# First pair of a DLRM tower cut into two quarters and a half, second pair at full width, no warming matmuls

## The reference, cut to what matters

```
x0 = e                                   # 512 x 32 x 16, gathered rows
for W in (W0, W1, W2):                   # W0: 32 x 32 x 64, the others 32 x 64 x 64
    xk = relu(einsum('bmd,bhd,mhk->bkd', x0, xk, W))
    outs.append(sum(xk, axis=2))
h = relu(concat(outs, dense_ctx) @ W_top1 + b_top1)      # 208 -> 512
y = relu(h @ W_top2 + b_top2) @ W_top3                   # 512 -> 256 -> 1
```

## Time and profile before

| what | value |
|---|---|
| median of three runs | 440.99 us |
| the profiled execution | 440.44 us |
| its span | 438.6 us |
| TensorE busy | 325.1 us (74%), 1892 passes |
| VectorE busy | 277.5 us (63%), 174 instructions |
| GpSimd busy | 259.6 us (59%), of it 122.1 in 128 gathers |
| ScalarE busy | 52.4 us (12%) |
| mean granted TensorE clock | 0.887 of full |

### The profile page before, as it was taken

How to read it: one execution, slowest core, us unless ns; L and a number is a source line. 1 busy time by engine, 2 the same in 40 slices (tenths; PEclk the granted TensorE clock), 3 DMA queues, 4 the chain that set the end, 5 groups by cost and what they waited for, 6 DMA issues and landing times.

```text
span 438.6 us, 4843 instructions
## 1 busy us (share of the span) xinstructions
PE 325.1 (74%) x1892; PEld 142.7 (33%) x1892; DVE 277.5 (63%) x174; ACT 52.4 (12%) x71; POOL 259.6 (59%) x199
## 2 busy tenths in 40 slices
PE   5500000028988999935989988998999999999997
PEld 5400000014544555612533332342233333223334
DVE  0000000005779797916899989999898897899911
ACT  1000000000000100100222211211022121121011
POOL 5777777500050000870788998889899878797200
PEclk9955555557999999985999999999999999999999
DMA  5356653000071000991497969897928998904000
GB/s 177 68 176 213 168 150 79 5 1 0 1 228 54 1 0 7 273 324 43 95 296 256 305 159 321 295 307 221 284 56 261 308 374 279 315 21 109 0 1 2
DMA packets 32529, 68.36 MB, mean 156 GB/s; under 512 B 5498, under 2 KB 12026, under 8 KB 32506
## 3 DMA queue, kind: packets, MB, share of 16 engines
q1 hardware_dynamic: 22074, 55.46, 38.1%
q10 hardware_dynamic: 6336, 11.54, 9.4%
q0 software_dynamic: 4096, 1.06, 2.9%
HBM read 54.40 MB, written 1.84 MB: 128 GB/s over the span
## 4 chain that ended last, share of the span: by engine, by line
PE 41%; another core or an unknown queue 22%; DMA 11%; issue 9%; DVE 7%; POOL 7%; ACTq 1%; SPq 1%; ACT 1%; DVEq 0%; POOLq 0%
PE acc L857 30%; DVE vz L659 7%; POOL pz L607 4%; PE factor L824 4%; DMA fields_sb<-fields 3%; POOL gathered L581 3%; DMA hidden<-relu_out 2%; PE factor L802 2%; DMA fields<-gathered 2%; DMA opposite<-fields 2%; DMA rotated<-fields 1%; PE factor L869 1%; ACTq L766 1%; PE factor L864 1%
## 5 line engine op out<-in xcount | busy, mean ns | idle before, releaser
L659 DVE TENSOR_TENSOR vz<-fields_sb,factor 128x1024 f32<-128x1024 f32 (+3 forms) x111 | 224.7, 2070 | 32.7 <-remote 12.9
L857 PE MATMUL acc<-vz,w_sb 128*64 128x512 f32 (+1 forms) x1200 | 225.5, 510 | 21.6 <-DVE vz L659 13.6
L607 POOL TENSOR_TENSOR pz<-fields_sb,hidden 128x1024 f32<-128x1024 f32 (+1 forms) x60 | 132.6, 2234 | 73.1 <-ACT hidden L738 59.7
L581 POOL DMA_INDIRECT gathered<-in_table,index x128 | 122.1, 954 | 72.7 <-DVE vz L670 37.4
L857 PEld LDWEIGHTS acc<-vz,w_sb 128*64 128x64 f32 x1200 | 85.6, 140 | 144.2 <-issue 103.1
L676 DVE TENSOR_TENSOR vz<-own,factor 128x512 f32<-128x512 f32 x8 | 5.5, 688 | 99.1 <-ACT own L730 92.5
L857 PE MATMUL acc<-pz,w_sb 128*64 128x512 f32 (+1 forms) x240 | 57.1, 566 | 2.8 <-POOL pz L607 2.8
L824 PE MATMUL factor<-gathered,unit_sb 32*128 32x128 f32 x32 | 4.2, 342 | 67.5 <-remote 65.9
L755 ACT ACTIVATE relu_out<-acc 128x512 f32<-128x512 f32 (+1 forms) x30 | 15.4, 513 | 146.0 <-PE acc L857 112.9
L724 ACT ACTIVATE factor<-hidden 128x1024 f32<-128x1024 f32 x22 | 22.6, 1028 | 72.0 <-DMA hidden<-relu_out 56.2
L857 PEld LDWEIGHTS acc<-pz,w_sb 128*64 128x64 f32 x240 | 17.3, 137 | 34.6 <-issue 23.9
(11 more groups left out here) (34 smaller groups left out, 63.5 us busy)
## 6 DMA issues: line engine op xcount, KB each, us to landing
fields_sb<-fields SPq DMA_DIRECT2D x48, 512.0 KB
rotated<-fields SPq DMA_DIRECT2D x24, 512.0 KB
hidden<-relu_out ACTq DMA_DIRECT2D x44, 256.0 KB
fields_sb<-fields SPq DMA_DIRECT2D x32, 256.0 KB
own<-fields SPq DMA_DIRECT2D x6, 512.0 KB
gathered<-in_table,index POOLq DMA_INDIRECT x128
fields<-gathered SPq DMA_DIRECT2D x12, 128.0 KB
w_sb<-in_w SPq DMA_DIRECT2D x2, 512.0 KB
```

What stands on the lines that cost most here:

```text
L581: nc.gpsimd.indirect_dma_start(gathered[:, pair % GRING, j, :], None, table, bass.IndirectOffsetOnAxis(ap=index[:, i:i + 1], axis=0)).then ...
L607: nc.gpsimd.tensor_tensor(pz[:, at % PRING, 0:cols], fields[s][:, t, col:col + cols], hidden_of(step, g), ALU.mult).then_inc(pz_ready, 1)
L659: nc.vector.tensor_tensor(vz[:, at:at + nt, 0:cols].rearrange("p t (a n) -> p t a n", n=half), src[:, t:t + nt, col:col + cols].rearrange( ...
L857: last = nc.tensor.matmul(acc_of(step, ab), w_sb[layer][:, kt, :], z[:, ab * half:(ab + 1) * half], start=start and j == 0, stop=stop and ...
```

## The change

It changes lists and constants, the table of factors of a direct block, and the order of the matmuls of the top.

- Pair 0 becomes three blocks: two of 256 columns (4 gathers each) and one of 512 (8 gathers). Pair 1 becomes one block of 1024 columns. There are still ten blocks and four direct ones.
- A direct block of 1024 columns has factor entries of its own, `[(OWN,), (0,), (1,), (2,), (3,), (ACROSS,)]`, and its layer 0 is five products of one tile. The entry that holds only `ACROSS` has no wave 0.
- `BEGUN`, `SPREAD`, `POOL_TILES`, `FIRST_GATHERS` and `GATHERS_IN` are written anew. POOL's tiles fall from 56 to 50, counted in tiles of 1024 columns.
- `WARMING` goes from 30 to 0 and `IN_FLIGHT_DIRECT` from 6 to 4.
- The top's matmuls that don't need layer 2 all come before the wait for `sums_done`, and the others follow in plain order.
- On the host the ids are laid out for the new blocks.

```diff
-BLOCKS = [(pair, half * N, N, half * GATHERS // 2, GATHERS // 2) for pair in range(2) for half in range(2)]
-BLOCKS += [(pair, 0, PAIR, 0, GATHERS) for pair in range(2, PAIRS)]
+BLOCKS = [(0, 0, N // 2, 0, GATHERS // 4), (0, N // 2, N // 2, GATHERS // 4, GATHERS // 4),
+          (0, N, N, GATHERS // 2, GATHERS // 2)]
+BLOCKS += [(pair, 0, PAIR, 0, GATHERS) for pair in range(1, PAIRS)]
...
-BEGUN = [(0, 0), (1, 0), (0, 1), (2, 0), (1, 1), (0, 2), (2, 1), (1, 2), (0, 3), (2, 2), (1, 3), (0, 4),
-         (2, 3), (0, 5), (1, 4), (1, 5), (0, 6), (2, 4), (2, 5), (0, 7), (1, 6), (1, 7), (2, 6), (0, 8),
+BEGUN = [(0, 0), (0, 1), (1, 0), (1, 1), (0, 2), (2, 0), (2, 1), (1, 2), (0, 3), (2, 2), (1, 3), (0, 4),
+         (2, 3), (0, 5), (1, 4), (1, 5), (0, 6), (2, 4), (0, 7), (2, 5), (1, 6), (1, 7), (2, 6), (0, 8),
          (2, 7), (0, 9), (1, 8), (1, 9), (2, 8), (2, 9)]
...
-SPREAD = [(1, 0), (2, 0), (1, 1), (2, 1), (1, 2), (2, 2), (1, 3), (2, 3), (1, 7)]
-POOL_TILES = {(1, 0): 0, (2, 0): 0, (1, 1): 0, (2, 1): 0, (1, 2): 0, (2, 2): 4, (1, 3): 0, (2, 3): 4,
-              (1, 4): 4, (1, 5): 4, (2, 4): 2, (2, 5): 4, (1, 6): 4, (1, 7): 4, (2, 6): 5, (2, 7): 6,
-              (1, 8): 6, (1, 9): 6, (2, 8): 4, (2, 9): 3}
-FIRST_GATHERS = 27
-GATHERS_IN = {(2, 2): (43, 0, 0, 1), (0, 4): (12,), (2, 3): (0, 1, 0, 0), (1, 4): (4, 2, 1, 0),
-              (1, 5): (1, 1, 0, 2), (0, 6): (3,), (2, 4): (1, 1), (2, 5): (5, 2, 3, 1), (0, 7): (5,),
-              (1, 6): (3, 1, 2, 1), (1, 7): (0, 4, 0, 0), (2, 6): (1, 0, 0, 0, 0)}
+SPREAD = [(1, 0), (1, 1), (2, 0), (2, 1), (1, 2), (2, 2), (1, 3), (2, 3)]
+POOL_TILES = {(1, 0): 0, (1, 1): 0, (2, 0): 0, (2, 1): 0, (1, 2): 0, (2, 2): 0, (1, 3): 0, (2, 3): 2,
+              (1, 4): 5, (1, 5): 2, (2, 4): 4, (2, 5): 4, (1, 6): 3, (1, 7): 2, (2, 6): 5, (2, 7): 6,
+              (1, 8): 4, (1, 9): 6, (2, 8): 4, (2, 9): 3}
+FIRST_GATHERS = 32
+GATHERS_IN = {(0, 4): (41,), (2, 3): (6, 0), (0, 5): (5,), (1, 4): (0, 1, 3, 0, 0), (1, 5): (4, 0),
+              (0, 6): (4,), (2, 4): (0, 1, 2, 1), (0, 7): (1,), (2, 5): (7, 0, 1, 0), (1, 6): (0, 0, 3),
+              (1, 7): (1, 8), (2, 6): (4, 3, 0, 0, 0)}
...
-WARMING = 30
+WARMING = 0
...
-IN_FLIGHT_DIRECT = 6
+IN_FLIGHT_DIRECT = 4
...
+            if BLOCKS[b][2] == PAIR:
+                return [(0, t, 1) for t in range(L0TILES + 1)]
             return [(0, 0, 1), (0, 1, 2), (0, 3, 1), (0, L0TILES, 1)]
...
-    units = [(0, t, 2) for t in range(0, TILES, 2)] if b in DIRECT else [(0, 0, 3), (0, 3, 3), (0, 6, 2)]
+    units = [(0, 0, 3), (0, 3, 3), (0, 6, 2)] if BLOCKS[b][2] == PAIR else [(0, t, 2) for t in range(0, TILES, 2)]
...
-            if spread_from_gathered(step):
+            if spread_from_gathered(step) and direct_factors(step[1])[g] != (ACROSS,):
...
-DIRECT_FACTORS = [(OWN, 0), (1, 2), (3, ACROSS)]
+def direct_factors(b):
+    if BLOCKS[b][2] == PAIR:
+        return [(OWN,), *((t,) for t in range(L0TILES)), (ACROSS,)]
+    return [(OWN, 0), (1, 2), (3, ACROSS)]
...
-            for m in range(F_TOP1 // P):
-                row = slice(m * HROWS, (m + 1) * HROWS)
-                nc.tensor.matmul(top1_bank(m), wt1_dense_sb[row, :], dense_sb[row, :], start=True, stop=False)
-            top1_first(0)
-            top1_first(1)
+            for m in range(F_TOP1 // P):
+                nc.tensor.matmul(top1_bank(m), wt1_sb[:, m * P:(m + 1) * P], stack01, start=True, stop=False)
+            for m in range(F_TOP1 // P):
+                row = slice(m * HROWS, (m + 1) * HROWS)
+                nc.tensor.matmul(top1_bank(m), wt1_dense_sb[row, :], dense_sb[row, :], start=False, stop=False)
             pe.wait_ge(sums_done, len(ORDER))
-            for ab in range(2):
-                top1_half(ab, ab).then_inc(top1_wave, 1)
-            top1_first(2)
-            pe.wait_ge(top1_wave, 2)
...
+            for m in range(0, F_TOP1 // P, 2):
+                for ab in range(2):
+                    top1_half(m + ab, ab).then_inc(top1_wave, 1)
+            for m in range(0, F_TOP1 // P, 2):
+                pe.wait_ge(top1_wave, m + 2)
+                for ab in range(2):
+                    top1_half(m + 1 - ab, ab).then_inc(top1_ps, 1)
...
```

More of the change, by code:

```diff
@@ L199, in factor_entry, with factor_entries, factor_used @@
     if spread_from_gathered(step):
[L200 removed]
+        g = next(e for e, held in enumerate(direct_factors(step[1])) if t in held)
     return step, g
[L205 to L209 removed]
+def factor_entries():
+    entries = []
+    for step, u in VECTOR:
+        if spread_from_gathered(step) and u == 0:
+            entries.append((step, 0))
+        entries.append(factor_entry(step, u))
+    return list(dict.fromkeys(entries))
+FACTORS = factor_entries()
+def factor_used(entry):
+    return max((i + 1 for i, (step, u) in enumerate(VECTOR) if factor_entry(step, u) == entry),
+               default=VECTOR.index((entry[0], 0)) + 1)
+FACTOR_USED = [factor_used(entry) for entry in FACTORS]
 def factor_free(entry):
@@ L421, in slot_of @@
         def slot_of(step, held):
-            g = next(e for e, of in enumerate(DIRECT_FACTORS) if held in of)
+            held_by = direct_factors(step[1])
+            g = next(e for e, of in enumerate(held_by) if held in of)
             half = BLOCKS[step[1]][2] // 2
-            at = DIRECT_FACTORS[g].index(held) * half
+            at = held_by[g].index(held) * half
             return factor[FACTORS.index((step, g)) % FRING][:, :, at:at + half]
@@ L678, in direct_product @@
                     return
-                both = factor[FACTORS.index((step, 1)) % FRING][:, :, :].rearrange("p a (t n) -> p t a n", t=2)
+                both = factor[FACTORS.index((step, 1)) % FRING][:, :, 0:2 * half].rearrange("p a (t n) -> p t a n", t=2)
                 nc.vector.tensor_tensor(vz[:, at:at + nt, 0:cols].rearrange("p t (a n) -> p t a n", n=half),
@@ L810, in spread_gathered @@
                 rows, quarter = quarter_rows(b), BLOCKS[b][2] // QUART
-                if wave:
+                if wave and (step, g) in WAVES:
                     pe.wait_ge(wave_done, WAVES.index((step, g)) + 1)
@@ L816, in spread_gathered @@
                         pe.wait_ge(vz_ready, factor_free((step, g)))
[L817 removed]
+                for held in direct_factors(b)[g]:
                     if held == ACROSS:
@@ new lines, in _ @@
+            for m in range(0, F_TOP1 // P, 2):
+                pe.wait_ge(top1_wave, m + 2)
+                for ab in range(2):
+                    top1_half(m + 1 - ab, ab).then_inc(top1_ps, 1)
+            for j in range(0, F_TOP1 // P, 2):
+                for k in range(j, j + 2):
+                    pe.wait_ge(top1_done[k], 1)
+                    last = nc.tensor.matmul(factor[2][:, 0, :], wt2_sb[:, k, 0:P], top1[:, k, :],
+                                            start=k == 0, stop=k == F_TOP1 // P - 1)
+                if j:
+                    last.then_inc(top2_ps, 1)
+                for h in range(2):
+                    for k in range(j, j + 2):
+                        last = nc.tensor.matmul(top2_bank(1, h), wt2_sb[:, k, P:2 * P], top1[:, k, half_batch(h)],
+                                                start=k == 0, stop=k == F_TOP1 // P - 1)
+                    if j:
+                        last.then_inc(top2_ps, 1)
@@ L953 @@
     ids = np.array(inputs["ids"]).reshape(PAIRS, QUART, GATHERS, FIELDS)
-    for pair in {BLOCKS[b][0] for b in DIRECT}:
-        ids[pair] = (ids[pair].reshape(2, 2, 2, GATHERS // 2, FIELDS).transpose(0, 2, 1, 3, 4)
-                     .reshape(ids[pair].shape))
+    samples = ids.reshape(PAIRS, 2, 2 * GATHERS, FIELDS)
+    ids = ids.copy()
+    for pair, _, _, j, rows in BLOCKS:
+        for q in range(QUART):
+            at = 2 * j + q % 2 * rows
+            ids[pair, q, j:j + rows] = samples[pair, q // 2, at:at + rows]
     ids = np.ascontiguousarray(ids.transpose(1, 3, 0, 2).reshape(P, PAIRS * GATHERS))
```

36 lines of the change are left out of this document (1 added, 35 removed).

## The result

The change makes the kernel **slower**: 450.34 us median of 4 runs (448.55 to 453.29) against 440.86 us (438.72 to 441.04), ratio 1.0233 with a 95% interval of 1.0163 to 1.0303. The profiled execution took 448.99 us, its span is 447.2 us (before 438.6).

The account below looks back on a forecast made before the run. It took the kernel as bound by a 97 us opening, where long rows of gathers delay TensorE's completions, then by TensorE, sharing with VectorE in 240 to 320 us. From 440.4 us, -5 - 4 + 2 + 2 = -5 gave 435, range 408 to 446.

Parts of the forecast that it names:

- Later gathers: Gathers after the first 64: rows of nine, six and five cost 6.5 in place of 10.4 us; -4, bounds -9 and +3.
- rival C: Nine gathers right after pair 0's layer 0 stall more, on small blocks: slower, 447 us, 452 at worst; chance 0.10.
- Warming: The 60 warming passes before any data: they cost nothing by themselves, so dropping them counts 0.
- Opening: First 97 us: completions still crawl, but the first quarter's layer 0 is nearly done by then; -5, bounds 0 and -20.
- blocks: Smaller and larger blocks in pairs 0 and 1: two quarters in place of a half; +2 us, bounds 0 and +6.
- head start: First block needs four gathers, not eight: TensorE starts at about 10.5 us, with about 59 passes by 97.1 us.
- Tiles to VectorE: Six full tiles moved from POOL cost VectorE 6.8 us, about half hidden: +2 us, bounds 0 and +6.8.
- Top: Matmuls before the wait for `sums_done`: same work in another order, 0, bounds -0.5 and +0.7 us.
- Rival A: TensorE runs freely during the gathers, work starting at 11 in place of 97 us: 365 us; chance 0.13.

Follow-up runs that it names:

- b_burst15b: On chip 1, kernel before with the row of 6 gathers after pair 0's layer 0 made 15 and the later 12 cut to 4: 441.29 us, 1.0060.
- b_warm0: On chip 1, the kernel before with WARMING = 0 and nothing else: 433.44 us, 0.9831 of the kernel before.
- experiment 2: Chip 1: kernel before again 441.41 us, changed kernel again 449.56, kernel before without warming 433.44, changed kernel with paced gathers 389.97.
- experiment 5: Chip 15: kernel before without warming and with paced gathers 345.28 us, changed kernel unchanged 352.14 us, against the kernel before at 343.98 us.
- before_copy: The kernel before, unchanged, run again on chip 1: 441.41 us, 1.0007 of the kernel before.
- after_copy: The changed kernel, unchanged, run again on chip 1: 449.56 us, 1.0193 of the kernel before.
- b_burst15: On chip 12, kernel before with the row of 6 gathers after pair 0's layer 0 made 15 and the later 12 cut to 4: 357.41 us, 1.0348.
- after_copy2: The changed kernel, unchanged, run on chip 15: 352.14 us, 1.0194 of the kernel before.
- a_late: On chip 14, the changed kernel with twelve of its last gathers moved earlier: 455.2 us, 1.0361 of the kernel before.
- b_pacelin_w0: On chip 1, the kernel before with WARMING = 0 and its gathers from the 17th to the 83rd paced by VectorE's products: 383.89 us, 0.8770.

## Why the prediction was wrong

The forecast was 435 us, in a range of 408 to 446; it came out at 450.34, slower and outside the range. By its own terms:

- **Later gathers: this is the step that failed.** Predicted: nine, six and five gathers at 4.5, 1 and 1 us, 6.5 in place of 10.4, so -4. What the earlier trace rows gave, 0.17 us per gather in a row of six and 0.78 in one of twelve, is not a price per gather. The row of six was nearly free; the row of twelve is 14.8 us long, and its step takes 13.0 us longer than on chip 15 (20.9 against 7.9); the two rows of nine and six are 19.1 us long together, and the kernel is 20.6 us late behind them. What eight or nine cost wasn't measured. And nine and six were counted as two rows. They are parted by one product of 0.73 us (132.24 us), and together they left TensorE idle 16.1 us. That the product doesn't part them is my reading of this one case; the unbroken fifteen of b_burst15b, 18.5 us long, made their step 13.5 us longer. In its place stands a balance: this row against the twelve at 184 us, 20.6 - 11.3 = 9.3 us for the worse by the third line, where the quarters' part is also in. I had the place right (rival C: the nine gathers after pair 0's layer 0, "where nine gathers cost over 6 us") but gave it 14 us at most and a chance of 0.10.
- **Warming: 0 predicted, -7.6 measured** (b_warm0). The prediction even said that the passes fill whatever holds completions back, and then priced that at nothing. If my reading of experiment 2 is right, sixty completions that nobody reads stand in the same line as those that matter. This is the gain of the kernel before; in the changed kernel the going of the warming wasn't tested alone, and the slow first passes of experiment 5 are its other side.
- **Opening -5 and blocks +2: -1.7 together.** With warming's -6.2 (124.2 us in before_copy, 118.0 in b_warm0, at the first line of the table) the quarters cost about +4.5 there, +5.7 in the repeat (before_copy and after_copy are 0.5 us apart), inside my bounds of 0 to +6 but not my +2. "Half of that and a part of its waits is saved" was wrong, since a quarter's layer 0 took as long as a half's. I had also read "80 to 76" instructions of VectorE for pairs 0 and 1: the lists give 70 products in both kernels, so the 0.6 us saved was nothing. The head start itself was seen: wave 0 started at 12.67 us, not at my 10.5, since the fourth gather's rows took 4.53 us to land and not 2.04. 24 passes were started by 17 us and 38 more by 84 us, 62 in all, then none until 96; my 59 by 97 us was nearly right. VectorE's first product came at 36.98 us, but the second at 59.76 and the third at 87.47.
- **Tiles to VectorE: right in size, nothing in time.** VectorE's busy time rose from 277.5 to 283.7 us, +6.2 for the 6.8 said, and POOL's fell by 15.2. Between the third and the fourth line of the table, where I had put +2, the kernel after is 4.2 us faster.
- **Top: 0 predicted, -0.7 measured**, inside the bounds.
- **Not foreseen: the last gathers.** +5.8 us at the step (+7.0 on chip 15), +3.9 at the end (+5.3), but only +0.5 in the repeat, after_copy against before_copy; some 3 us by the medians of experiment 5. The last gather comes 8 us later, and I had looked at the rows only, not at what waits for the last of them. The chain behind it (copy to DRAM, `rotated`, fields of block 8) was there to be read in the code.

Rival A, free running, and the Trainium skill's rule behind it (SBUF — State Buffer, Who interferes with whom) need a remark. On chips 12 and 15 the trace agrees with it: 79 and 73 gathers in a row (b_burst15, after_copy2), TensorE at nine tenths for most of it. In the first result and on chips 1 and 14 it doesn't: 11.83 and 8.46 us of waiting for nobody beside fifteen gathers (11.52 and 8.47 in after_copy, 11.71 and 8.49 in a_late), gone when they are spaced out. Whether what is held back there has to do with the ports that this section is about, no run shows. And rival A wouldn't have paid even where it holds, since there the kernel before runs freely too.

## What to carry to other kernels

When a wait grows with a row of other instructions, price the whole row as it will stand after the change, with rows parted by a short product counted as one until shown otherwise, and not by a mean per instruction; and set it against the row that goes. When work is reordered, follow the last item of each list to who needs it. A smaller first block pays only if its passes get cheaper, so price them from rows at the speed that TensorE has there; here the spreading passes did not, and the whole of it ran at the slow pace. The version that held on both kinds of chip is the kernel before without warming and with its gathers spaced by waits: 0.877 where there are stalls and 1.0036 where there are none.

## What the runs showed of the hardware

- The same program takes 344 us on two chips and 440 us on three (if the first result's is a third), with intervals of a few us. The difference is the stall beside indirect gathers. What differs between the chips is open. One thing goes with it in all runs: on chips 12 and 15 the profile has the landing times of the full tiles of `fields_sb` (5.6 to 6.5 us) and of the gathers (3.6 to 4.5 us), and on chips 1 and 14, as in the first result, it has none for them. It goes with the kind of chip; nothing here says that it is a cause.
- Whether the held-back thing is TensorE's completion, or the semaphore's update, or the wait's release, wasn't told apart: each shows as a late release of VectorE.
- On a stalling chip the paced gathers still cost: b_pacelin_w0 takes 383.89 us there and 345.28 us on chip 15. The row of twelve stays whole in it (127.66 to 141.45 us) and VectorE waits 9.00 us beside it; block 3's layer 1 takes 20.0 us there and 7.9 on chip 15. So 12 of these 39 us are that stall. How the rest divides between stall and waiting wasn't tried further.
- Warming isn't worth the same on both kinds of chip. On chip 15, without it, b_pacelin_w0b ends its first relu at 25.4 us; on chip 12, with it and with the same eight gathers ahead, b_burst15 does at 22.0 us. The passes show why: eight of layer 0's last take 1.07 us without warming (23.93 us) and 0.61 us with it (20.97 us). On chip 1 its going brought 7.6 us in all; there TensorE starts no pass for 66 us behind the first wave (22.2 to 88.2 us in before_copy), and the same eight passes take 1.07 us with it or without it. The mean granted clock went up with its going, from 0.888 (before_copy) to 0.979 (b_warm0), so on this chip that mean says little of the speed of the work.
- The column of the granted clock and the speed of the passes can disagree: in the kernel after it has 1.00 at 98 to 104 us, where passes of 128 columns come 0.107 us apart, and 1.00 at 106 to 114 us, where they come 0.054 us apart.
